# One VectorE maximum over sixteen heads in place of two over eight, with the older image's normalising behind it

## The reference, cut to what matters

```
h   = token mixing: a softmax over the 4 groups weighs and adds them      # 16 x 128 x 256
h   = h + attention(layernorm(h))    # 16 heads of 16, causal, softmax(scores / 4)
h   = h + moe(layernorm(h))          # shared expert + 6 of 64 experts for each token
```

```
scores = einsum('bqhd,bkhd->bhqk', Q, K);  scores = where(causal, scores, -inf)
probs  = softmax(scores / sqrt(hd))                    # needs the maximum of each row and head
out    = einsum('bkhd,bhqk->bqhd', V, probs) @ W_o.T + b_o
```

## Time and profile before

| | |
|---|---|
| median of 3 runs | 507.87 us (506.15 to 508.51) |
| profiled execution | 504.11 us, of which the span of the trace is 502.3 us |
| busy in the span | PE 431.6 us, DVE 321.6, POOL 246.4, ACT 215.0 |
| mean granted PE clock | 0.954 of 2.4 GHz |
| image loop | first maximum at 33.8 us, last scatter issued at 251.8 us |
| expert tiles | first matmul at 259.1 us |

### The profile page before, as it was taken

The page is one execution under the profiler, slowest core; times in us unless marked ns, Lnnn a source line. Parts: engine busy times, 40 slices in busy tenths (PEclk is TensorE's granted clock), DMA queues, the critical chain, the costliest instruction groups (busy, mean ns, idle before and its releaser), DMA issues.

```text
span 502.3 us, 13166 instructions
## 1 busy us (share of the span) xinstructions
PE 431.6 (86%) x3950; PEld 332.4 (66%) x3950; DVE 321.6 (64%) x1065; ACT 215.0 (43%) x662; POOL 246.4 (49%) x273
## 2 busy tenths in 40 slices
PE   1567889888988999778379999999999999976995
PEld 1446667666767776453258888888888888852653
DVE  3675789999899998877613444444444444430998
ACT  3254755564555556332014454454544544530000
POOL 1111115767666678767714656665565565560000
PEclk9988999998999999998769999999999999995999
DMA  8999971112111211222235687677577747643997
GB/s 273 336 351 296 302 210 54 66 65 77 65 64 59 73 66 65 87 85 85 105 105 164 197 244 256 185 213 240 177 237 232 232 138 221 215 132 106 409 407 271
DMA packets 56476, 90.00 MB, mean 179 GB/s; under 512 B 7719, under 2 KB 43690, under 8 KB 56400
## 3 DMA queue, kind: packets, MB, share of 16 engines
q1 hardware_dynamic: 44016, 61.69, 39.8%
q0 software_dynamic: 10080, 25.29, 14.2%
q10 hardware_dynamic: 2304, 2.10, 1.2%
HBM read 84.00 MB, written 40.82 MB: 248 GB/s over the span
## 4 chain that ended last, share of the span: by engine, by line
PE 27%; issue 8%; POOL 6%; DMA 5%; DVE 3%; SPq 1%; POOLq 0%; DVEq 0%
PE ps_low L1059 14%; PE ps L1059 8%; POOL y_rows L423 6%; PE ps_low L1305 3%; DMA x_sb<-y_rows 2%; DMA y_rows<-y,xring 2%; PE ps L1292 2%; DVE x_sb L816 1%; DVE x_sb L1037 1%; DVE x_sb L1054 1%; DMA slot_rows<-xring,slot_ix 1%; DVE h_all L1042 1%; DVE x_sb L1047 0%; DMA xring<-slot_rows 0%; POOL slot_rows L393 0%
## 5 line engine op out<-in xcount | busy, mean ns | idle before, releaser
L423 POOL DMA_INDIRECT y_rows<-y,xring x114 | 112.1, 984 | 89.7 <-issue 82.9
L1059 PE MATMUL ps_low<-wring,probt 128*128 x456 | 119.4, 385 | 0.0
L1020 DVE TENSOR_TENSOR probt<-probt,ps_low 128x128 f32<-128x128 f32 x114 | 32.7, 287 | 108.7 <-issue 89.5
L1059 PEld LDWEIGHTS ps_low<-wring,probt 128*128 128x128 f32 x456 | 78.8, 193 | 6.3 <-issue 0.2
L1059 PE MATMUL ps<-wring,probt 128*128 x228 | 68.2, 382 | 0.0
L560 ACT COPY probt<-ps_low 128x256 f32<-128x256 f32 x115 | 42.8, 372 | 49.3 <-PE ps_low L1305 48.3
L1013 DVE TENSOR_SCALAR y<-ps,xring 128x256 f32<-128x256 f32 x114 | 54.6, 479 | 6.4 <-DMA y_rows<-y,xring 5.1
L393 POOL DMA_INDIRECT slot_rows<-row,slot_ix x48 | 51.8, 1079 | 13.9 <-issue 13.4
L393 POOL DMA_INDIRECT slot_rows<-xring,slot_ix x48 | 51.6, 1076 | 14.0 <-issue 13.7
L565 ACT ACTIVATE probt<-ps_low 128x128 f32<-128x128 f32 x114 | 31.6, 277 | 58.0 <-PE ps_low L1059 58.0
L475 ACT ACTIVATE probt<-ps_low 128x512 f32<-128x512 f32 x64 | 33.1, 603 | 40.9 <-PE ps_low L1059 40.9
(11 more groups left out here) (184 smaller groups left out, 731.5 us busy)
## 6 DMA issues: line engine op xcount, KB each, us to landing
wring<-wexp SPq DMA_DIRECT2D x115, 384.0 KB
xring<-slot_rows SPq DMA_DIRECT2D x115, 129.0 KB, 2.5
x_sb<-y_rows SPq DMA_DIRECT2D x16, 768.0 KB, 6.5
slot_rows<-pads SPq DMA_DIRECT2D x1, 8256.0 KB, 35.2
x_sb<-x SPq DMA_DIRECT2D x3, 2048.0 KB, 18.0
slot_rows<-pads SPq DMA_DIRECT2D x5, 516.0 KB, 9.9
x_sb<-x SPq DMA_DIRECT2D x4, 512.0 KB, 5.1
out<-h_all ACTq DMA_DIRECT2D x16, 128.0 KB, 5.4
```

Source lines behind the costliest of these rows:

```text
L423: nc.gpsimd.indirect_dma_start(out=y_dram, out_offset=bass.IndirectOffsetOnAxis(ap=xring[:, q, TO_AT:TO_AT + 1].bitcast(I32), axis=0), in_ ...
L1020: nc.vector.tensor_tensor(hm[:, t % 2, :], silu[:, t % 2, :], psS[t % 2][:, INTER:2 * INTER], ALU.mult).then_inc(S("h_ready"), 1)
L1059: return nc.tensor.matmul(*a, **k)
```

## The change

The two calls of `nmax_of` become one, at the place of the first, over all four banks: 16 maxima of 128 elements for each partition in one instruction instead of 8 and 8. `den_of`, the first token-mixing product, `place(0)`, and in four steps `hidden` or `shift`, and then `normalise` follow it. Nothing of the arithmetic changes; `shift_of` counts one semaphore increment less for each image. The other engines' programs are the same.

```
-            def nmax_of(b, half):
+            def nmax_of(b):
                 dve.wait_ge(S("scores_done"), b + 1)
-                two = slice(2 * half, 2 * half + 2)
-                nc.vector.tensor_reduce(nmax[:, two, :], ps_low[:, two, :].rearrange("p g (a k) -> p g a k", a=GH),
+                nc.vector.tensor_reduce(nmax[:], ps_low[:].rearrange("p g (a k) -> p g a k", a=GH),
                                         axis=AX, op=ALU.max, negate=True).then_inc(S("shift_parts"), 1)
...
-                dve.wait_ge(S("shift_parts"), 3 * b + 2 + part)
+                dve.wait_ge(S("shift_parts"), 2 * b + 1 + part)
...
                 if has(b):
-                    nmax_of(b, 0)
+                    nmax_of(b)
                 if has(cc):
                     den_of(cc)
                 mixed(0)
                 placed(0)
...
                 if has(cc):
                     normalise(cc)
-                if has(b):
-                    nmax_of(b, 1)
                 placed(1)
```

## The result

| | before | after |
|---|---|---|
| median of 4 runs each, us | 507.01 (504.96 to 508.51) | 533.42 (532.60 to 540.84) |
| profiled execution, us | 504.11 | 533.95 |
| span of the trace, us | 502.3 | 532.2 |
| mean granted PE clock | 0.954 | 0.912 |

The ratio of the times is 1.0531, with a 95% interval of 1.0486 to 1.0576; runs more than 1.5% above the fastest of the same kernel, such as the 540.84 here and the profiled one of experiment 2, are left out of the ratios. By the medians the changed kernel is slower by 26.4 us.

What follows compares the result with a forecast made beforehand. DVE was taken to bound most steps, PE's chain having 0.30 us of slack. Longer chain 9 us plus clock falls 13.5 gave 22.5 us, on 504.11 or 507.87 us; forecast 528 us, range 513 to 536.

Steps and rivals of the forecast that it cites:

- One reduction for two: DVE's maxima: one merged instruction takes about 2.28 us, shortening DVE's own step by only about 0.07 us.
- `normalise` behind the whole of it: On DVE: `o_sb` ends 3.20 us behind the maximum's start, 1.07 later; PE's transposes to projection shrink to 1.50 us.
- The sum for a step: Image-loop step: the chain through PE and DVE becomes 12.14 us, longer than DVE's 11.42, and bounds every step.
- The sum for the loop: Image loop: the longer chain costs 14 steps together 9 us, about 0.9 each in six chain-bound steps.
- rival B: Image loop: the chain grows but PE's clock holds; price 9 us, 513 to 517 us, chance 0.27.
- The clock: PE in the image loop: longer waits bring 10 clock falls instead of 1, 1.5 us each, 13.5 us in all.
- Rival C: Image loop: DVE stays the bound, so no loss or a gain of 1.1 us, 503 to 507 us; chance 0.10.
- Rival D: DVE's reduction merges badly, 2.43 us or more, adding 2 us to the forecast or the chain-only case; no separate chance.

Runs made afterwards that it cites:

- experiment 2: The kernel before, with its two half reductions kept separate but both put ahead of `normalise`: median 533.13 us, ratio to before 1.0499; also called number 2.
- number 3: The changed kernel plus three needless PE matmuls in PE's wait for `o_sb` in each of 14 steps: median 514.60 us, ratio to before 1.0136.
- number 5: The kernel before, with the maxima split into three banks ahead of `normalise` and one behind, instead of two and two: 512.98 us, ratio 1.0108.

## Why the prediction was right

The forecast was slower, by a longer chain and by falls of the clock, 528 us in a range of 513 to 536. It came out at 533.4, for these two reasons. The size of the second was low: in the profiled executions the loop grew by 29.4 us, where the sum had 22.5.

- *One reduction for two*: right. 2.28 us were estimated, 2.292 measured. Two reductions one behind the other take 2.35 us in number 2, so one saves 0.06 us, by the seam as said. The Trainium skill's page "VectorE: DVE Perf Modes" (section on the TRN2 errata) has a fixed term by which, as an estimate, 0.125 us would be saved here; the runs show half of that.
- *`normalise` behind the whole of it*: right. `o_sb` ends 3.27 us behind the maximum's start (3.20 said). From the transposes to the projection it is 1.43 us at full clock (number 3: 162.09 to 163.52; 1.50 said). PE's waits for `o_sb` are 28.7 us (28 said), of 1.9 to 2.0 in a usual step, but not all are longer than any before, as was said: in step 4 it is 1.49.
- *The sum for a step*: right. 12.14 said, 12.10 in number 3. In the changed kernel the steps shown take 13.5 us, since they have a fall.
- *The sum for the loop*: right. 9 us said, 8.0 by medians and 10.1 by the loops' lengths. Steps 3 and 13, taken as bound by the chain, were to pay about 0.9 us each, and pay 0.91 and 0.92. With the clock held, rival B's price is what is measured: 514.6, within its 513 to 517.
- *The clock*: the price of a fall was right, the number of falls too small. In the step shown the fall adds 0.45 us from the transposes to the projection (177.06 - 175.18 = 1.88 instead of 1.43) and 0.88 from there to the end of the scores (185.12 - 177.06 = 8.06; number 3: 170.70 - 163.52 = 7.18), together 1.33 us, where 1.5 was said. A loop of 193.41 us at a mean of 0.87 has some 50 us at the lower level ((1 - 0.87) / 0.5 x 193.41), before some 3. That is about 15 stretches of 3.4 us instead of one, where I had taken 10. Its term measures 19 us instead of 13.5, which is the upper bound that was kept for it (19.5). The 10 was a choice between two bounds and rested on one wait of 1.58 us that was followed by a fall; two waits of 1.72 us in the same trace, the one in the earlier trace rows and the one at 213.87 below, were not. So it was in part luck that the choice went to the right side. The Trainium skill's page "TensorE: Matmul & The Clock Gate" (section "HAM oscillation") describes loops that pay the lower level in every round. The trace comes near to that, with the lower level in 12 of 14 steps.

```profile
213.87 0.41 PE L1184 MATMUL ps<-const_sb,row 128*128 128x128 f32 x2 [1.72 <-DVE o_sb L721]
```

- Rival C is out: no middle step comes near 11.4 us except step 13 (11.86), which took 10.94 before. `shift_b` ends 0.47 us behind `o_sb` (175.50 and 175.03; 0.46 said), and PE reaches it without a wait. Rival D is out with 2.292 us.
- The delay passes to the end whole: the expert stage takes 243.3 us, 243.2 before.

## What to carry to other kernels

Before an instruction is moved ahead of another on a full engine, look for who waits for the one that is pushed back, and whether that wait is for its data or for a buffer that it still reads; a free bank took away 22 of 26 us here. Where TensorE waits in every step, ask two prices: the longer chain, and the lower clock behind the wait, which here was the larger; a few matmuls in the wait that compute nothing tell the two apart in one run. An order that serves two consumers, half of the work on either side of the other output, can be better than either order with the work in one piece.

## What was not expected of the hardware

The loop does not recover by itself: in 12 of 14 steps there is a fall, mostly with 3.4 us at 1.2 GHz, and in the steps shown the clock is back at 2.4 GHz ahead of the next wait, at 13.5 us a step (the windows of the changed kernel). Filling some 1.3 us of a wait of 2 us (1.99 - 0.68) was enough to keep 0.99 through the loop (number 3).

Yet neither the length of one wait nor the total says which steps fall. Two waits of the changed kernel, in steps 3 and 4:

```profile
77.89 0.41 PE L1181 MATMUL ps<-const_sb,row 128*128 128x128 f32 x2 [2.34 <-DVE o_sb L720]
...
90.68 0.66 PE L1181 MATMUL ps<-const_sb,xring 128*128 128x128 f32 x2 [1.49 <-DVE o_sb L720]
```

The 2.34 us brought no fall (0.41 for the two transposes, and 1.00 in the window of this step); at the end of the 1.49 us the clock was already down (0.66). What decides it stays open. As for the total: PE waits 20.7 us for `o_sb` in the loop of number 5, at most 2.1 in one step, and has a mean clock of 0.97; with 27.8 us, at most 2.6, it is 0.87 in the changed kernel.
